# Relation products begun behind the norm of five tiles instead of all twenty-five

## What is computed

```python
x = x + _L0_gnn_ref(_layernorm(x), L0_gnn_weight, edge_weight1, src, dst, edge_type_16)

def _L0_gnn_ref(h, weight, norm, src, dst, rel_type):
    transformed = jnp.einsum('ni,rio->rno', h, weight)      # 16 relations, 256 x 256 each
    msg = transformed[rel_type, src] * norm
    return jax.ops.segment_sum(msg, dst, num_segments=h.shape[0])
```

## Time and profile before

| | |
|---|---|
| median of 3 runs | 2680.85 us (2680.56 to 2688.63) |
| span of the profiled execution | 3179.1 us |
| PE, PEld busy | 1968.0, 1556.4 us |
| DVE, ACT, POOL busy | 1545.2, 927.1, 1402.9 us |
| first product (L421) | 30.58 us |
| last product's end | 310 us |

### The profile page before, as it was taken

One profiled execution on the slowest core, in us unless ns is written; L12 is line 12 of the kernel. 1 busy time (PEld: TensorE's weight loads), 2 busy tenths in 40 slices (PEclk: granted clock), 3 DMA queues, 4 the chain that ended last, 5 costly groups with the idle time before them and its releaser, 6 DMA issues.

```text
span 3179.1 us, 37685 instructions
## 1 busy us (share of the span) xinstructions
PE 1968.0 (62%) x10259; PEld 1556.4 (49%) x10259; DVE 1545.2 (49%) x4920; ACT 927.1 (29%) x2035; POOL 1402.9 (44%) x1415
## 2 busy tenths in 40 slices
PE   7998344353367999734555564564365455555599
PEld 6887233243237999623443343443244344344377
DVE  4200133233276555634564564575365555566853
ACT  4443576673013444320111111113011111111432
POOL 1000666666603443245555555513555555553143
PEclk9999676666678999876776766787576776677799
DMA  6444565554238999743344344323333443442000
GB/s 215 187 199 192 171 210 187 193 196 141 87 88 279 353 355 351 240 149 117 104 127 124 100 130 124 100 69 104 109 120 117 117 120 116 119 122 88 1 14 28
DMA packets 207421, 473.85 MB, mean 149 GB/s; under 512 B 33230, under 2 KB 100370, under 8 KB 200750
## 3 DMA queue, kind: packets, MB, share of 16 engines
q0 software_dynamic: 63520, 179.35, 20.0%
q1 hardware_dynamic: 112878, 190.07, 16.7%
q10 hardware_dynamic: 30816, 101.99, 9.0%
HBM read 367.19 MB, written 104.90 MB: 148 GB/s over the span
## 4 chain that ended last, share of the span: by engine, by line
another core or an unknown queue 29%; PE 29%; DVE 27%; issue 10%; DVEq 3%; POOL 1%; DMA 1%; ACT 1%; SPq 0%; POOLq 0%; ACTq 0%
PE banks L421 9%; PE banks L1256 7%; DVE arena L1661 3%; DVE arena L1745 3%; PE banks L1268 3%; DVE arena L825 3%; DVE X L834 2%; DVE arena L1710 2%; DVEq L696 2%; DVEq L699 1%; PE banks L1422 1%; DVE xn L1673 1%; POOL arena L1463 1%; PE banks L2164 1%
## 5 line engine op out<-in xcount | busy, mean ns | idle before, releaser
L1463 POOL DMA_INDIRECT arena<-ht,srcT x784 | 783.7, 1000 | 696.7 <-DVE arena L1745 400.8
L783 POOL DMA_INDIRECT arena<-tr,idx1T x392 | 376.5, 961 | 398.3 <-DMA tr<-arena 207.9
L1572 PE MATMUL banks<-arena,XT 128*128 128x264 f32 x884 | 392.6, 536 | 229.1 <-DVE arena L1745 148.5
L811 PE MATMUL banks<-arena 128*128 x884 | 257.1, 454 | 327.0 <-DVE arena L825 258.1
L811 PEld LDWEIGHTS banks<-arena 128*128 128x128 f32 x884 | 196.2, 229 | 388.0 <-issue 356.1
L1572 PEld LDWEIGHTS banks<-arena,XT 128*128 128x128 f32 x884 | 213.2, 260 | 296.8 <-DVE arena L1745 158.5
L1573 PE MATMUL banks<-arena,XT 128*128 128x264 f32 x884 | 358.0, 496 | 0.0
L1745 DVE TENSOR_TENSOR arena<-arena,nrmT 128x528 f32<-128x528 f32 x442 | 309.9, 703 | 20.8 <-ACT nrmT L1519 12.4
L834 DVE TENSOR_TENSOR X<-X,banks 128x256 f32 x221 | 92.6, 419 | 395.3 <-remote 367.6
L421 PE MATMUL banks<-parts 128*128 128x512 f32 x1200 | 275.1, 391 | 4.7 <-DVE parts L381 4.7
L1573 PEld LDWEIGHTS banks<-arena,XT 128*128 128x128 f32 x884 | 228.5, 259 | 58.8
(11 more groups left out here) (366 smaller groups left out, 3284.0 us busy)
## 6 DMA issues: line engine op xcount, KB each, us to landing
arena<-in_L_ffn_w_dram SPq DMA_DIRECT2D x195, 512.0 KB
tr<-arena SPq DMA_DIRECT2D x50, 1024.0 KB, 3.9
XT<-otd ACTq DMA_DIRECT2D x52, 512.0 KB
arena<-ohd ACTq DMA_DIRECT2D x52, 512.0 KB
arena<-dld ACTq DMA_DIRECT2D x28, 512.0 KB
otd<-arena ACTq DMA_DIRECT2D x28, 512.0 KB
ohd<-arena ACTq DMA_DIRECT2D x28, 512.0 KB
arena<-ht,srcT POOLq DMA_INDIRECT x784
```

The costliest lines, as they stand in the source:

```text
L783: pool.indirect_dma_start(Gr[:, o:o + D], None, TR, bass.IndirectOffsetOnAxis(ap=idx1T[:, q:q + 1], axis=0)).then_inc(d_g[b % NG], 16)
L811: mm = ten.matmul(B[n][:, 0:D], OHr[:, n, h, :], Gr[:, h * D:][:, bass.ds(o, D)], start=(h == 0), stop=(h == 1))
L1463: pool.indirect_dma_start(Gall[:, o:o + ROW], None, HT[L], bass.IndirectOffsetOnAxis(ap=srcT[:, q:q + 1], axis=0)).then_inc(d_g[b % NG], 16)
L1572: ten.matmul(B[n][:, 0:MSG], OH[b][:, 2 * j, :], WG[:, j, 0, :], start=True, stop=False)
```

## The change

*Order of transfers.* SyncE loads group 0 of x, then the eight weight transfers, then groups 1 to 4 of x, then the `dst` rows (`sp_x(0, 1)`, `sp_weights`, `sp_x(1, NGR)`, `sp_ahead`).

*Norm.* `dve_norm`, `pe_norm` and `act_norm` are not used for the first norm any more (they are for the later ones). New functions do one group: statistics, root, reciprocal, normalised tiles. Group 0 comes first, groups 1 and 2 between tiles 0 and 1, groups 3 and 4 between tiles 1 and 2. Turned tiles go through two banks, 6 and 7.

*Weights.* ScalarE casts each of the four weight groups between the copies of `XT` tiles 0 to 4, and VectorE makes all four low parts. GpSimd's subtraction is gone.

*Check of the order of the edges.* Its memsets and comparison move behind the norm of group 4 on VectorE (`dve_ahead`).

```diff
-        def sp_x():
-            for g in range(NGR):
+        def sp_x(g0, g1):
+            for g in range(g0, g1):
...
+        def turned0(i):
+            return B[6 + i % 2]
...
+        def dve_norm0(g):
+            vec.wait_ge(d_x[g], 32 if g == NGR - 1 else 16)
+            tiles = range(g * GT, g * GT + GT)
+            st = []
+            for i in tiles:
+                if i >= 10 and i % GT == 0:
+                    vec.wait_ge(mv_ok, MV[LN0] + i - 5)
+                st.append(dv.put(vec.bn_stats(bns[:, i % 10, :], X[:, i, :])))
+            for n, i in enumerate(tiles):
+                vec.wait_ge(dv.sem, st[n])
+                vec.bn_aggr(mv[:, i, :], bns[:, i % 10, :]).then_inc(mv_ok, 1)
+            vec.wait_ge(sq_ok, MV[LN0] // GT + g + 1)
+            rs = rstd[:, g * GT:(g + 1) * GT]
+            vec.wait_ge(dv.sem, dv.put(vec.reciprocal(rs, rs)))
+            for i in tiles:
+                if i > 3:
+                    vec.wait_ge(tp_ok, LN0 + i - 3)
+                vec.tensor_scalar(xn[:, i % 4, :], X[:, i, :], mv[:, i, 0:1], rstd[:, i:i + 1], ALU.subtract,
+                                  ALU.mult).then_inc(xn_ok, 1)
+
+        def pe_norm0(g):
+            for i in range(g * GT, g * GT + GT):
+                ten.wait_ge(xn_ok, LN0 + i + 1)
+                if i > 1:
+                    ten.wait_ge(xt_ok, LN0 + i - 1)
+                src = xn[:, i % 4, :]
+                ten.transpose(turned0(i)[:, 0:P], src[:, 0:P], ident[:, :])
+                ten.transpose(turned0(i)[:, P:2 * P], src[:, P:2 * P], ident[:, :]).then_inc(tp_ok, 1)
+
+        def act_root0(g):
+            act.wait_ge(mv_ok, MV[LN0] + (g + 1) * GT)
+            act.activation(rstd[:, g * GT:(g + 1) * GT], mv[:, g * GT:(g + 1) * GT, 1], ACT.Sqrt,
+                           bias=epsc[:, 0:1]).then_inc(sq_ok, 1)
+
+        def act_norm0(i):
+            act.wait_ge(tp_ok, LN0 + i + 1)
+            act.copy(XT[:, :, i * P:(i + 1) * P],
+                     turned0(i)[:, 0:2 * P].rearrange("p (k c) -> p k c", k=2)).then_inc(xt_ok, 1)
...
         def act_weights():
+            act_root0(0)
+            act_norm0(0)
             for g in range(4):
                 q = slice(4 * g, 4 * g + 4)
                 act.wait_ge(d_w[g], 32)
                 act.copy(whi[:, :, q, :], wraw[:, :, q, :]).then_inc(wh_ok, 1)
+                act_norm0(g + 1)
...
         def dve_weights():
-            vec.memset(onesw, 1.0).then_inc(k_ok, 1)
-            vec.memset(ones0, 1.0).then_inc(k_ok, 1)
-            for i in range(NX - 1):
-                dve_rows(i)
-            for g in (0, 1, 3):
+            dve_rows(0)
+            for g in range(4):
...
+            dve_rows(1)
...
-            q = slice(8, 12)
-            pool.wait_ge(wh_ok, 3)
-            pool.tensor_tensor(wlo[:, :, q, :], wraw[:, :, q, :], whi[:, :, q, :].bitcast(F32), ALU.subtract).then_inc(k_id, 1)
...
-                if i == 0:
-                    if j == 5:
-                        ten.wait_ge(xt_ok, LN0 + NT)
-                    if j == 4:
-                        ten.wait_ge(k_id, LOW2)
-                    elif j % 2 == 0:
-                        ten.wait_ge(wl_ok, (1, 2, 0, 3)[j // 2])
+                if i == 0 and j % 2 == 0:
+                    ten.wait_ge(wl_ok, j // 2 + 1)
...
             for i in range(NT):
                 act_rows(i)
+                for g in later_norms(i):
+                    act_root0(g)
+                    for t in range(g * GT, g * GT + GT):
+                        act_norm0(t)
+
+        def later_norms(i):
+            return range(2 * i + 1, 2 * i + 3) if i < 2 else ()
 
         def pe_transform():
+            pe_norm0(0)
             for i in range(NT):
                 pe_rows(i)
+                for g in later_norms(i):
+                    pe_norm0(g)
+                if i == 1:
+                    ten.wait_ge(xt_ok, LN0 + NT)
                 pe_tables(i)
 
         def dve_transform():
             for i in range(NT):
                 if i + NX - 1 < NT:
                     dve_rows(i + NX - 1)
+                for g in later_norms(i):
+                    dve_norm0(g)
+                if i == 1:
+                    dve_ahead()
                 dve_tables(i)
...
         def _(eng):
-            sp_x()
+            sp_x(0, 1)
             sp_weights()
+            sp_x(1, NGR)
+            sp_ahead()
```

More of the change, by code:

```diff
@@ L183, in build @@
         CONST, PADS, ONES, WORSE, FLAG, FIRSTS, DIAG, SHIFT, ZEROS = 6, 9, 11, 12, 13, 14, 16, 17, 18
-        IDENT, UPPER, LOW2 = 1, 2, 3
+        IDENT, UPPER = 1, 2
         d_x = sems("d_x", NGR)
@@ L208, in dve_const @@
             vec.wait_ge(k_ok, CONST)
-        def sp_x():
-            for g in range(NGR):
+        def sp_x(g0, g1):
+            for g in range(g0, g1):
                 t0, t1 = g * GT, min(g * GT + GT, NT - 1)
                 sync.dma_start(X[:, t0:t1, :], a["x"][t0 * P:t1 * P, :].rearrange("(t p) d -> p t d", p=P)).then_inc(d_x[g], 16)
+            if g1 < NGR:
+                return
             sync.wait_ge(k_ok, 1)
@@ L285, in act_norm @@
                     then(i)
-        def dve_norm0():
-            dve_norm(LN0, lambda g: vec.wait_ge(d_x[g], 32 if g == NGR - 1 else 16))
+        def turned0(i):
[35 more added lines that the diff above has]
+                     turned0(i)[:, 0:2 * P].rearrange("p (k c) -> p k c", k=2)).then_inc(xt_ok, 1)
         base0 = top[0]
@@ L356, in sp_weights, with sp_ahead @@
                                    a["L0_gnn_weight"][q, k * P:(k + 1) * P, :].rearrange("r p d -> p r d")).then_inc(d_w[g], 16)
+        def sp_ahead():
             sync.dma_start(ahead[0], a["dst"].rearrange("(p j) -> p j", j=RL)).then_inc(d_ch, 16)
@@ L381, in dve_weights, with dve_ahead @@
                 vec.tensor_tensor(wlo[:, :, q, :], wraw[:, :, q, :], whi[:, :, q, :].bitcast(F32), ALU.subtract).then_inc(wl_ok, 1)
+            dve_rows(1)
+        def dve_ahead():
+            vec.memset(onesw, 1.0).then_inc(k_ok, 1)
+            vec.memset(ones0, 1.0).then_inc(k_ok, 1)
             vec.wait_ge(d_ch, 64)
@@ L428, in act_rows @@
             if i == 0:
-                act.wait_ge(wl_ok, 3)
-                act.wait_ge(k_id, LOW2)
+                act.wait_ge(wl_ok, 4)
             for j in range(8):
@@ L764, in pool_gather @@
         def pool_gather():
+            pool.wait_ge(k_id, UPPER)
             pool.wait_ge(tb_ok, 1)
@@ L2331, in _ @@
             act.wait_ge(k_ok, CONST)
-            act_norm(LN0)
             act_weights()
@@ L2360, in _ @@
             ten.wait_ge(k_id, IDENT)
-            pe_norm(LN0)
             pe_transform()
@@ L2388, in _ @@
             dve_pads()
-            dve_norm0()
+            dve_norm0(0)
             dve_weights()
```

## The result

| | before | changed |
|---|---|---|
| median of 7 runs | 2680.85 us (2679.91 to 2688.63) | 2693.03 us (2689.16 to 2698.75) |
| ratio to before, 95% interval | | 1.0036 (1.0024 to 1.0047) |
| span of the profiled execution | 3179.1 us | 2691.3 us |
| first product | 30.58 us | 17.02 us |
| first product of tile 2 | 54.15 us | 60.33 us |

What follows compares the result with a forecast made beforehand. TensorE was taken to bound the relation stage from its first product; 20.6 us (9.9 + 10.7) of insertions plus 4.0 for the clock less 12.4 gained gave +12.2 us, 2693.0 us, 0.45% slower, range 2684 to 2700.

Steps and rivals of the forecast that it cites:

- slow starts: Products of tiles 1 and 2 begin at the lower clock behind the moved norms, losing 2.0 us each, bounds 0 to 2.8.
- The sum: Whole change: 20.6 us of waits between tiles plus 4.0 of lower clock less 12.4 gained at tile 0's end, +12.2 us.
- One of its signs: Sign to look for in the trace: tile 2's products begin 10 to 14 us later than 54.2 us.
- Start of the products: TensorE's first product at about 18.0 us against 30.58, bounds 16.4 and 21.
- The gate: Before the first product, tile 4 waits for XT of tile 2, behind the cast of weight group 1: 15.5 + 1.9 + 0.4 us.
- Insertions: Norms of groups 1 and 2 between tiles 0 and 1 cost 9.9 us, groups 3 and 4 between tiles 1 and 2 10.7.
- five tiles through two banks: First group's transposes and copies between row tiles: 1.31 us for two tiles, the fifth's XT written after 3.7 us.
- VectorE's statistics, which I had called hidden: Between row tiles: 1.74 + 0.34 us for five tiles fit inside, group 1's before 30 us, group 2's beside the copies.
- Clock: TensorE's granted clock falls during both blocks of norm work between tiles and thin transposes don't bring it back; 4.0 us lost.
- the rival of the holding clock: Thin transposes keep TensorE at 2.4 GHz between tiles, no product starts slowly: +6.7 us, 2687.5; chance 0.20.
- the Trainium skill's rule: Idle gaps between TensorE bursts lower the clock; to the letter, thin work isn't idle, the clock holds, the sum is 6.7.
- Passing the shift through whole: Behind the relation stage, the gather waits for its write to `tr`, so the stage's +12.2 us reach the end unscaled.

Runs made afterwards that it cites:

- x_first: Changed kernel with the old order of transfers, all of x and then the weights; ratio to the kernel before 1.0076.
- two_first: Against the kernel turning later tiles behind product banks: only tiles 0 and 1 turned before the first product, 2 to 4 behind tile 0's first banks; ratio to before 0.9965.
- roots_early: Changed kernel with both groups' statistics ahead of their normalised tiles and both square roots ahead of the row tile's last eviction; ratio to the kernel before 0.9987.
- the interleaved kernel: Changed kernel with tiles 5 to 24 turned one behind each bank of products, roots and statistics early, edge tables two row tiles later; ratio to before 0.9957.
- before_again: The kernel before, unchanged, run once more; ratio to before 1.0006.
- clock_fill: Changed kernel with 14 throwaway transposes ahead of the transposes of each of groups 1 to 4; ratio to the kernel before 1.0016.

## Why the prediction was right

**The sign and its cause, right.** TensorE's pauses moved from ahead of its bound stage into it. With the terms as measured: 13.6 us gained at the first product (30.58 to 17.02), 18.3 lost in two pauses (8.98 and 9.79 between product starts, less two ordinary distances of 0.23), and 3.5 lost to slow starts, sum +8.2; the last product came 8.5 us later. The sum had 20.6 + 4.0 - 12.4. One of its signs failed: tile 2 was to begin 10 to 14 us later than before and began 6.2 us later (60.33 against 54.15). With a start 1.1 us better at the end of tile 0 than forecast, pauses 2.3 us shorter and 0.5 us less lost to slow starts, each term of the sum forecast too great a loss, by 4 us together.

**Start of the products: 18.0 forecast, 17.02 measured.** The gate was as described, tile 4 behind the cast of weight group 1, and x_first and two_first show both halves of it. Weights came sooner: the casts of groups 1 to 3 began at 14.39, 16.87 and 19.90 us, where I had the landings at 15.5, 18.6 and 21.7. I moved them up by x's bytes at 335 GB/s, 7.6 us; against x_first, with x ahead of them, the last cast begins 9.1 us earlier (29.0 to 19.90).

**Insertions: 9.9 and 10.7 forecast, about 9.0 and 9.8 measured.** The step that was too long is "five tiles through two banks" of the first group in each: I gave it 3.7 us with transposes at the lower rate, but the clock was still full there (1.00 from 29.5 to 34.2 us), and from the first transpose (31.43) to the end of ScalarE's last copy (34.20) it was 2.8 us; the second group's five, at the lower level, took 3.5 us (35.71 to 39.23). VectorE's statistics, which I had called hidden, then held the second root until 34.67, 0.5 us of the gain. A passage from a root to the first transpose took 1.0 us instead of 1.25. roots_early, which leaves 5 to 5.7 us, shows what of it the roots' chains cost; the rest is the pace of ten tiles through two banks, 0.48 us a tile, where the interleaved kernel pays 0.24 for the two transposes.

**Clock: right in kind.** It fell in both insertions, in the second half, and the transposes there did not bring it back. (The argument for that, that those of 10 to 26 us had not, holds for the first profile alone: in before_again the clock rose at the end of such transposes, too late for them to use it.) The slow starts lasted 3.7, 2.7 and 4.8 us; at a rate of 0.427 against 0.227 us for a product they lost 1.7, 1.3 and 2.2 us, where I took 2.0 each. clock_fill isolates it: with the clock held, the last product comes 4.9 us earlier, 3.5 of them from the two slow starts and 1.4 from faster transposes in the pauses. Its gather comes 2.7 to 3.6 us behind those of the two profiles of before, where the rival of the holding clock had 6.7: that sum had the same too long pauses and the same too late start in it. Of the Trainium skill's rule ("TensorE: Matmul & The Clock Gate", "HAM oscillation — how this bites in real kernels"), read to the letter, the trace disagrees: the clock fell in insertions where no single wait of TensorE for `xn` was longer than 1.9 us. That bursts behind such gaps start slowly agrees, with 2.7 and 4.8 us here.

**What hid the miss.** The stage lost 8.2 us by the terms (8.5 by the last product, 7.6 against before_again) and not 12.2; the median moved by 12.2, the ratio by 9.7 (interval 6.4 to 12.6). So the point was hit partly by luck, the scatter of the runs. Passing the shift through whole agrees with the traces: seven of the eight in the table take 2364.0 to 2371.4 us behind the first gather, whether that comes at 307.5 or at 324.2 us (the eighth, x_first, takes 2375.2). Their scatter is as wide as the shift, so no single pair of them would show it.

## What to carry to other kernels

An engine that bounds a stage should start early only if it can then run on: work that hid in its wait ahead of the stage costs, put between its bursts in a block, the whole round trip over the other engines, here 9 us for 2 to 4 us of transposes. Spread over the burst, one small piece behind each bank, the same work cost its bare 0.24 us a tile, and the early start (the order of the loads, above all) then paid: 0.43% faster than before. Ask of every moved block what each of its waits is for, and issue those producers ahead of the burst's last eviction.

## What the runs showed of the hardware

The same kernel's products began at half the rate for 3.6 us in one profile and for 5.6 us in another, after the same 4.7 us without work and at the same place; in the second the clock rose as the last transposes ended and fell again 3.4 us later, before any product could use it. So a burst after a pause has a cost, here 1.7 and 2.6 us, that varies between executions of one program, and a trace's stage times are good to about 1 us.

Twenty-eight transposes into an unused bank held the granted clock at 1.00 through a pause of 8 us; in both pauses together that earned 4.9 us in the traces, 0.2% in the ratios (1.0036 to 1.0016). Shorter pauses, 5 us with 21 instructions in them, held it too.

The first profile's column of the clock reads 1.00 for the first 34 us, while the durations (643 against 389 ns) say half the rate. There the durations are the ones to believe.
